# Grouped attention as one stream over four sequences: 64-row score pairs, shared score and projection banks, output projection in the stream

## The reference, cut to what matters

```python
h = _rms(x, ln_w)
q = (h @ wq).reshape(B, S, 32, 64)
k = (h @ wk).reshape(B, S, 8, 64)
v = (h @ wv).reshape(B, S, 8, 64)
q, k = _rope(q, k)                  # t1,t2 halves of 32: q*cos + [-t2,t1]*sin
k, v = repeat each of the 8 heads 4 times
scores = einsum('bqhd,bkhd->bhqk', q, k) / sqrt(64)
scores = where(causal, scores, -1e30)
attn = softmax(scores, -1)
o = einsum('bhqk,bkhd->bqhd', attn, v).reshape(B, S, 2048)
x = x + o @ wo
```

## Time and profile before

| | us |
|---|---|
| median of 3 runs | 3047.16 |
| range of the runs | 3040.61 to 3047.91 |
| the profiled execution's own time | 3039.91 |
| its span, first to last instruction | 3038.1 |
| grouped attention, from 682.0 to 1695.9 | 1013.9 |
| one sequence of it (start to start) | 253.6 |
| one unit inside a sequence | 11.91 |

### The profile page before, as it was taken

How to read it: one execution, slowest core, us unless ns; L and a number is a source line. 1 busy time by engine, 2 the same in 40 slices (tenths; PEclk the granted TensorE clock), 3 DMA queues, 4 the chain that set the end, 5 groups by cost and what they waited for, 6 DMA issues and landing times. The chain is left out here.

```text
span 3038.1 us, 44303 instructions
## 1 busy us (share of the span) xinstructions
PE 2452.8 (81%) x12088; PEld 1662.4 (55%) x12088; DVE 1693.3 (56%) x5549; ACT 1243.7 (41%) x3486; POOL 1324.6 (44%) x1245
## 2 busy tenths in 40 slices
PE   6999999938998998999899589952657485599992
PEld 6888888934555555556455466531323233277661
DVE  7666666655653662663565343328645656653334
ACT  3444444434542552553454244321445253433331
POOL 3444444414552551553454158862220302117885
PEclk9999999979999999999999789986688796889996
DMA  4000000020000000000000635550000000224554
GB/s 153 15 14 14 14 14 14 5 80 1 1 2 1 2 1 2 1 1 2 1 1 1 227 61 86 86 130 0 1 1 0 0 0 0 112 74 84 86 86 111
DMA packets 72733, 112.48 MB, mean 37 GB/s; under 512 B 11648, under 2 KB 59520, under 8 KB 72128
## 3 DMA queue, kind: packets, MB, share of 16 engines
q0 software_dynamic: 30336, 42.73, 8.7%
q1 hardware_dynamic: 37968, 63.15, 5.9%
q10 hardware_dynamic: 4224, 4.19, 0.4%
HBM read 80.69 MB, written 36.32 MB: 39 GB/s over the span
## 5 line engine op out<-in xcount | busy, mean ns | idle before, releaser
L1017 POOL TENSOR_TENSOR b_sm<-b_sm,b_rden 128x128 f32<-128x128 f32 (+3 forms) x512 | 363.4, 721 | 267.1 <-DVE b_rden L985 257.7
L927 ACT ACTIVATE b_sm<-b_sm,b_mn 128x128 f32<-128x128 f32 (+3 forms) x512 | 286.3, 559 | 349.0 <-DVE b_mn L979 349.0
L848 PEld LDWEIGHTS b_t<-ident,b_sm 128*128 128x128 f32 x1280 | 156.0, 141 | 221.1 <-issue 120.1
L839 PE MATMUL b_s<-b_k,b_q 128*128 128x128 f32 (+3 forms) x688 | 254.1, 454 | 21.8 <-POOL b_q L1004 21.8
L848 PE MATMUL b_t<-ident,b_sm 128*128 128x128 f32 x1280 | 229.7, 278 | 43.3 <-POOL b_sm L1017 30.6
L979 DVE CUSTOM_DVE_ANT_0 b_sm<-b_s,maskB 128x128 f32<-128x128 f32 (+3 forms) x344 | 167.1, 486 | 148.6 <-issue 147.7
L1380 POOL DMA_INDIRECT XN<-rows,m_slots x158 | 158.2, 1001 | 94.0 <-issue 47.6
L409 POOL TENSOR_TENSOR a_q<-a_prod 128x512 f32<-128x512 f32 x64 | 81.8, 1278 | 229.0 <-DVE a_prod L355 229.0
L1962 DVE TENSOR_REDUCE c_nm<-c_first 128x2 f32<-128x1024 f32 x128 | 149.7, 1217 | 35.1 <-PE c_first L1753 35.1
L825 PE MATMUL b_pj<-b_h,b_w 128*128 128x512 f32 x320 | 161.9, 594 | 0.0
L860 PE MATMUL b_o<-b_pt,b_v 128*64 128x512 f32 (+3 forms) x1024 | 157.3, 450 | 3.9 <-DVE b_pt L971 3.9
(11 more groups left out here) (288 smaller groups left out, 5826.7 us busy)
## 6 DMA issues: line engine op xcount, KB each, us to landing
WM<-in_m_w_dram SPq DMA_DIRECT2D x4, 3072.0 KB, 17.0
WM<-in_m_w_dram SPq DMA_DIRECT2D x4, 2432.0 KB, 14.0
acc<-in_zeros_dram SPq DMA_DIRECT2D x3, 2176.0 KB, 15.5
n_part<-acc SPq DMA_DIRECT2D x12, 512.0 KB, 7.1
a_wa<-in_a_wa_dram SPq DMA_DIRECT2D x8, 512.0 KB, 4.6
b_w<-in_b_w_dram SPq DMA_DIRECT2D x1, 3072.0 KB, 9.8
XN<-rows,m_slots POOLq DMA_INDIRECT x158, 2.8
X<-in_x_dram SPq DMA_DIRECT2D x4, 512.0 KB, 5.7
```

Source lines behind the costliest of these rows:

```text
L839: pe.matmul(p_s[g % 3][:, 0:keys(t)], q_r[:, m % 2, t * P:(t + 1) * P], kp[:, m // B_REP % 2, head, 0:keys(t)], start=True, stop=True).the ...
L848: x = pe.transpose(p_t[g % 2][:, k * P:(k + 1) * P], sm[:, g % RING, k * P:(k + 1) * P], c.ident[:, :])
L927: act.activation(sm[:, g % RING, 0:keys(t)], sm[:, g % RING, 0:keys(t)], ACT.Exp, scale=-1.0, bias=mn[:, g % RING:g % RING + 1], accum_out ...
L1017: pool.tensor_tensor(sm[:, s, 0:keys(t)], sm[:, s, 0:keys(t)], rden[:, s:s + 1].to_broadcast([P, keys(t)]), ALU.mult).then_inc(s_pn, 1)
```

## The change

`attention1` is written anew around **steps**: a step S is one query tile of both heads, a unit M four steps (j = 0 to 3, tiles 0, 2, 1, 3), and all 256 steps are one unrolled stream over the four sequences.

- The heads of a pair stand side by side (a in rows 0 to 63, b in 64 to 127), by another layout of the weights and of `b_sin`. Scores are matmuls over 64 rows of q and k; `rowsB`, `pad` and the padded copies go.
- Rotating swaps blocks of 32 rows: one product by cos and four by sin, of 32 rows each.
- Four PSUM banks (`front`) go round between scores and all projections: a use waits until the fourth use before it has been read. Two (`back`) go round between transposes and values. Two (`p_y`) collect the output projection.
- PE transposes step S - 2; ACT copies step S - 3, both heads, and DVE copies none. ACT also takes v out of PSUM.
- q is projected, rotated and added two units ahead, the next pair's k in units 1, 5, 9, 13 (four of 16) and the next sequence's v tiles in units 6, 8, 10, 12, beside the stream.
- Values and output projection of unit M - 2 come in unit M; `out_proj` adds a unit's share to the sum in two halves of 2 tiles. The sum of a sequence goes into XN in two additions.
- The copy of HT goes: PE reads `c.HT`. `Y` holds v (two sequences) instead of half of `ot`; `prod` has two buffers, q three, the row ring `sm` eight as before.

```diff
-        p_proj, p_s, p_t = [pb("pj0"), pb("pj1")], [pb("s0"), pb("s1")], [pb("t0"), pb("t1")]
-        p_o, p_y = pb("o"), pb("y")
-        p_s.append(p_y)
+        front, back = [pb(f"f{i}") for i in range(4)], [pb(f"t{i}") for i in range(2)]
+        p_y = [pb("y0"), pb("y1")]
...
+                def front_free(use):
+                    if FRONT[use] < 4:
+                        return
+                    kind, i, n = earlier = fronts[FRONT[use] - 4]
+                    if kind == "s":
+                        pe.wait_ge(s_mn, 2 * i + n + 1)
+                    elif kind == "v":
+                        pe.wait_ge(s_vc, i * TB + n + 1)
+                    else:
+                        pe.wait_ge(s_prod, ROPES[earlier] + 1)
...
-                    pe.matmul(p_s[g % 3][:, 0:keys(t)], q_r[:, m % 2, t * P:(t + 1) * P],
-                              kp[:, m // B_REP % 2, head, 0:keys(t)], start=True, stop=True).then_inc(s_sc, 1)
+                    for head in range(2):
+                        front_free(("s", S, head))
+                    for head in range(2):
+                        r = slice(head * B_HD, (head + 1) * B_HD)
+                        pe.matmul(front_bank(("s", S, head))[:, 0:keys(t)], q_r[r, M % 3, t * P:(t + 1) * P],
+                                  k_r[r, pg % 2, 0:keys(t)], start=True, stop=True).then_inc(s_sc, 1)
...
+                for S in range(LAST):                     # PE
+                    M, j = S // STEPS_OF, S % STEPS_OF
+                    turns, ends = 0 <= S - TURN_LAG < TOTAL, 0 <= M - 2 < UNITS
+                    if S < TOTAL:
+                        scores(S)
+                    if j == 0 and ends:
+                        values(M - 2)
+                    if j == 0 and M + 2 < UNITS:
+                        project(("q", M + 2, 0))
+                    if j == 1 and beside(M) is not None:
+                        project(beside(M))
+                    if j == 2 and ends:
+                        out_proj(M - 2, 0)
+                    if turns:
+                        transposes(S - TURN_LAG)
+                    if j == 3 and ends:
+                        out_proj(M - 2, 1)
...
+                for S in range(LAST):                     # ACT
+                    M, j = S // STEPS_OF, S % STEPS_OF
+                    if 0 <= S - COPY_LAG < TOTAL:
+                        copy_pt(S - COPY_LAG)
+                    if S < TOTAL:
+                        exp(S)
+                    if j == 0 and 0 <= M - 2 < UNITS:
+                        copy_out(M - 2)
+                    if j == 1 and beside(M) is not None and beside(M)[0] == "v":
+                        copy_v(beside(M))
...
-                    dve.scalar_tensor_tensor(prod[0:r, 1, :], bank[r:P, :], scale, sin[r:P, :], ALU.mult, ALU.mult)
-                    dve.scalar_tensor_tensor(prod[r:P, 1, :], bank[0:r, :], scale, sin[0:r, :], ALU.mult,
-                                             ALU.mult).then_inc(s_prod, 1)
+                    dve.scalar_tensor_tensor(to[:, 0, :], bank[:, :], scale, cos[:, :], ALU.mult, ALU.mult)
+                    for at in range(4):
+                        src, dst = slice(at * h, (at + 1) * h), slice((at ^ 1) * h, ((at ^ 1) + 1) * h)
+                        x = dve.scalar_tensor_tensor(to[dst, 1, :], bank[src, :], scale, sin[src, :], ALU.mult, ALU.mult)
+                    x.then_inc(s_prod, 1)
...
+                for S in range(TOTAL + 1):                # DVE
+                    M, j = S // STEPS_OF, S % STEPS_OF
+                    if S < TOTAL:
+                        minimum(S)
+                    if S >= 1:
+                        inverse(S - 1)
+                    if j == 0 and M > 2 and M % B_UNITS == 2:
+                        add_y(M // B_UNITS - 1)
+                    if j == 0 and M + 2 < UNITS:
+                        rotate(("q", M + 2, 0))
+                    if j == 1 and beside(M) is not None and beside(M)[0] == "k":
+                        rotate(beside(M))
...
+                for S in range(TOTAL + 1):                # POOL
+                    M, j = S // STEPS_OF, S % STEPS_OF
+                    if S >= 1:
+                        normalise(S - 1)
+                    if j == 1 and M + 2 < UNITS:
+                        add(("q", M + 2, 0))
+                    if j == 2 and beside(M) is not None and beside(M)[0] == "k":
+                        add(beside(M))
```

More of the change, by code:

```diff
@@ L857, in values @@
+                def values(M):
+                    b = M // B_UNITS
+                    if M % B_UNITS == 0:
+                        pe.wait_ge(s_vc, (b + 1) * TB)
+                    pe.wait_ge(s_pt, (M + 1) * 2 * STEPS_OF)
+                    back_free(("o", M, 0))
+                    bank = back_bank(("o", M, 0))
+                    pair = M % B_UNITS // B_REP
                     for k in range(TB):
```

408 lines of the change are left out of this document (188 added, 220 removed).

## The result

| | kernel before | changed kernel |
|---|---|---|
| median of the runs | 3046.5 us (3040.6 to 3047.9, 4 runs) | 3074.0 us (3073.3 to 3076.7, 4 runs) |
| ratio | 1 | 1.0096, 95% interval 1.0078 to 1.0113 |
| span of the profiled execution | 3038.1 us | 3074.6 us |
| grouped attention within it | 1013.9 us | 1047.5 us |

The changed kernel is slower by 27.5 us in the medians and by 36.5 us in the profiled executions, 33.6 of them in the grouped attention (682.0 to 1729.5, where the last addition of y ends). The other 2.9 us lie behind it, where nothing was changed.

A forecast was written before the change was run, and what follows sets the result against it. TensorE bounded the old kernel; a chain through all engines would bound the new. Start 24.2, rounds 938.8 and rest 43.4 give 1006, with clock 1024 against 1013.9 us: 10 slower, 3047.2 + 10 = 3057 us, range 2995 to 3122.

The forecast's parts named there:

- a chain through all engines: From one q projection's end to the next: rotation, tile 2's exps, copies, transposes, scores of tile 3, values, projection; 14.84 us.
- k round: A round in the 4 of 16 units that also project and rotate k; forecast 17.04 us.
- the clock: TensorE's granted clock falling to 1.2 GHz after waits: nine of ten k units, 1.0 us each, 13.5 us; 4 elsewhere.
- plain rounds: Rounds of the grouped attention's units without k or v work, 34 of 61; forecast 14.84 us each.
- v rounds: Rounds in the 4 of 16 units with v work, 12 of 61; forecast 15.32 us each.
- hand-overs: Passing work from one engine to the next, eleven on the round; for example 0.21 us PE to DVE, 0.05 before values.
- The first rival: The chain is shorter than summed, by hand-over errors or 32-row products of 0.35 us; about 3025 us, chance 0.34.
- The v step: ScalarE's copy of v, 0.48 us, stands before the copies of tile 3 in v units, making the round 15.32.
- The k step: In k units a second rotation of 3.53 us stands before the minima of tile 1, making the round 17.04.
- The third rival: The clock falls in nearly every unit: 46 more rounds at 1.4 us, 64 us more, 3121 us; chance 0.14.
- GpSimd's path: GpSimd's products for tile 2, head b, and TensorE's work behind them end 0.2 us before the chain, so barely hidden.
- the fourth rival: The chain isn't tight and TensorE's own work, 12.2 us a unit, sets the pace; 2860 us, chance 0.02.

The follow-up runs named there:

- e1_rot64: Changed kernel with the rotation's four VectorE products of 32 rows made into two of 64 rows; span 2945.0 us against 3074.6.
- e3_twice_t3: Changed kernel with the score pair of tile 3 (512 keys, both heads) issued twice; span 3126.2 us against 3074.6.
- e9_copies_first: Changed kernel with ScalarE's two copies of tile 3's blocks moved ahead of tile 2's exps; span 3029.5 us against 3074.6.
- e4_twice_t2: Changed kernel with the score pair of tile 2 issued twice, with 512 columns; span 3077.3 us, stage 1046.4 against 1047.5.
- e5_fill: Changed kernel with one extra score matmul of tile 3 in TensorE's wait for k's rotation, in 15 units; span 3060.2 us against 3074.6.
- e8_values_late: Changed kernel with q's projection ahead of values, tile 0's reciprocals before q's rotation, values behind scores of tile 2, their output's copy before tile 2's exps; span 2912.4 us.
- e11_values_late_k: e8_values_late with, in 15 k units, k's projection ahead of values and the output's copy behind tile 2's exps; span 2897.5 us against 2912.4.

## Why the prediction was right, and where its sum was off

Direction and mechanism held: slower, because a chain through all engines replaced TensorE's own pace, with the rotation (e1_rot64), scores of tile 3 (e3_twice_t3) and ScalarE's copies (e9_copies_first) on it and scores of tile 2 (e4_twice_t2) off it. The forecast was 10 us more and 3057; measured are 27.5 more in the medians and 3074, 2.7 times the difference. The 10 us were barely more than the 9 that the prediction called no change, and it gave slower only 0.47; that the direction held owes something to luck. The sum against the trace (a k round without the clock is taken as 17.04, which two of the 15 have, and the clock as what all 15 have above it):

| term | forecast | measured |
|---|---|---|
| start to the first q rotation | 24.2 | 21.3 |
| 34 plain rounds (the first without values) | 502.0 | 516.7 |
| 12 v rounds | 183.8 | 189.1 |
| 15 k rounds without the clock (the forecast takes the first without values) | 253.0 | 255.6 |
| clock | 17.5 | 17.3 in k rounds |
| rest of the stage | 43.4 | 47.6 |
| stage | 1024 | 1047.5 |

- **The hand-overs** are the term that was mis-sized, 20 of the 24 us. In each plain and v round 0.43 us were missing. By the timeline of the plain round, counted from the rotation's start: the minimum starts at 3.63 instead of 3.53; the exps add nothing to that (4.23 for 4.13), nor do the copies (5.44 for 5.35). The second transpose of tile 0 starts at 6.64 instead of 6.46, and scores of tile 3 at 6.87 instead of 6.63. Values start at 10.95 instead of 10.60, q's projection at 13.25 instead of 12.92, the next rotation at 15.27 instead of 14.84. Three times a round TensorE waits for a copy on ScalarE, and 0.145 us passed each time from the copy's end to the matmul's start (for values: the copy starts at 1081.77 and takes 0.47, values start at 1082.39). The prediction had 0.05 for this step and no row behind it; that is about what the earlier trace rows give for VectorE to ScalarE. Two of the three lie on the chain, so this makes 0.19 of the 0.43. The rest is 0.10 between the rotation and the minimum, 0.06 between the transposes and scores of tile 3, and 0.11 in q's projection, which takes 1.82 from its start to its last column (1.98 in the row, less 0.165 of filling and draining) where the sum has 1.71. With some hundredths the other way this is the 0.43. Why these three are longer no run shows. The first rival spoke of errors of 0.05 a hand-over that would shorten the round; over eleven of them they were 0.04 each, with the other sign.
- **The v step** (0.48 for ScalarE's copy of v) was exact, 15.76 against 15.28. **The k step** was too: 17.04 forecast and 17.04 in the two rounds without a fall. There the chain runs through k's rotation and not through ScalarE's copies, which carry the error of the plain round. That both agree to the last digit is luck in part, since the other hand-overs are in it as well.
- **The clock** had 13.5 us in k units and 4 elsewhere. In the trace it is 17.3 in k rounds, in 13 of 15, 1.3 each, and the granted clock is at its full level through all plain and v rounds but the first (0.72 there). The sum was right, its split was not: 1.3 a fall for 1.0, and nothing for the 4 elsewhere. That 17.5 and 17.3 agree is luck in part. e5_fill shows the cause. The third rival (falls in nearly every unit) is out.
- **First units and end.** The prediction took values out of the first two rounds, but only the first has none: the second (from 715.56, 17.67 long) has those of unit 0 at 728.90. This is the 2.6 us in the k rounds' row. The first was 3.0 us shorter (12.28), though the clock is low in much of it. The last two units without a rotation took 11.9 each instead of 11, and the end behind them 15.8 instead of 13.5. The start was 2.9 us shorter than I had it.
- **GpSimd's path** lay 0.7 us behind the chain, not 0.2. It cost the forecast nothing, since it stayed hidden in the plain rounds.
- **The rivals.** The first had its deciding point at a mean round of 15.2 without clock. Measured is 15.76 (978.7 less 17.3, by 61). Its premise of 0.35 for 32-row products is refuted (687 ns). What spoke against it, that nothing on the chain can pass its neighbour in the queue, is what decided; with the order changed TensorE does set the pace (e8_values_late, e11_values_late_k), the fourth rival's case, but busy for 12.7 us a round and not 12.2.
- **The medians** differ by less than the spans (27.5 and 36.5 us): the profiled execution of before (3039.9) lies 6.6 us under the median of its runs, that of the changed kernel (3076.7) 2.7 above its own. Another 2.9 us of the spans' difference are the scatter behind the stage.

## What to carry to other kernels

When work is moved into one stream, count what the slowest engine does, and then walk once around from a step to its next occurrence through every queue: if this is longer than the work (15.28 against 11.97 in a plain round here), it is the time. Then look for the step on that round that stands behind another by program order alone. Here q's projection stood behind values and ScalarE's copies behind exps; moving such steps was worth 5.8% of the kernel's time, once the next path behind it was treated too, and a step that gives nothing alone (the early reciprocals) may give 0.58 us a round after another one.

## What the runs showed of the hardware

- One matmul of 0.96 us in a wait of 1.41 us kept the granted clock at its full level in 14 of 15 places, with waits of 0.82 and 0.22 us still there, while a wait of 1.37 us in each plain round caused no fall. The fall had cost 1.3 us each time, more than the matmul.
- A VectorE product of 32 rows and 512 columns takes 687 ns, one of 64 rows 689: in this kernel a product costs the same whatever its rows, so splitting one by rows multiplies its cost.
- Two fp32 matmuls of 64 rows run side by side: 0.93 us from pair to pair for 512 columns.
- From the end of a ScalarE copy to the matmul that waits for its bank 0.145 us passed, about 0.1 more than from VectorE to ScalarE.
